# The order of helper calls in the eight attention turns, the last MLP and the recurrence periods, with the first and last rounds as functions of their own

## The reference

```python
x = L0(x, ctx)     # attention over channels, 64x64 weights, relu, residual
for w in (L1, L2): # two transformer layers
    q, k, v = split(layernorm(x) @ w_qkv + b_qkv)
    x = x + merge_heads(softmax(scores(q, k) * mask - 1e4 * (1 - mask)) @ v) @ w_ao + b_ao
    q = layernorm(x) @ w_q + b_q
    k, v = split(ctx @ w_kv + b_kv)
    x = x + merge_heads(softmax(scores(q, k) * cross_mask ...) @ v) @ w_co + b_co
    x = x + gelu(layernorm(x) @ w1 + b1) @ w2 + b2       # 256 -> 1024 -> 256
# L3: a recurrent block
xn = layernorm(x); sx = shifted(xn) - xn
x5 = xn + sx * (maa + tanh((xn + sx * maa_x) @ maa_w1) @ maa_w2)   # five mixes
w = exp(-exp(time_decay + tanh(x5[1] @ decay_w1) @ decay_w2))
r, k, v, g = x5[3] @ Wr, x5[0] @ Wk, x5[2] @ Wv, silu(x5[4] @ Wg)
s[t] = k[t] v[t]^T + w[t] * s[t-1];  out[t] = r[t] (u * k[t] v[t]^T + s[t-1])
x = x + groupnorm(out) * g @ Wo
x = x + sigmoid(xr @ ffn_Wr) * (relu(xk @ ffn_Wk)^2 @ ffn_Wv)
```

## Time and profile of the kernel before

| | us |
|---|---|
| three runs | 1107.12, 1105.58, 1101.60 |
| median | 1105.58 |
| the profiled execution | 1112.12 |
| its span in the trace | 1110.3 |
| granted clock of TensorE, mean of the span | 0.966 |

### The profile page before, as it was taken

The page is one execution under the profiler, slowest core; times in us unless marked ns, Lnnn a source line. Parts: engine busy times, 40 slices in busy tenths (PEclk is TensorE's granted clock), DMA queues, the critical chain, the costliest instruction groups (busy, mean ns, idle before and its releaser), DMA issues. The chain is left out here.

```text
span 1110.3 us, 24267 instructions
## 1 busy us (share of the span) xinstructions
PE 1022.3 (92%) x9312; PEld 697.3 (63%) x9312; DVE 772.5 (70%) x1517; ACT 517.6 (47%) x996; POOL 434.8 (39%) x387
## 2 busy tenths in 40 slices
PE   6998899999999999999999999998986889989966
PEld 4775676678677677677677678674462453644524
DVE  3674869757757757757757757754458898896964
ACT  4663463662662662662662662651411534414331
POOL 2111545443443443443443443431326536275240
PEclk9998899999999999999999999999998999989998
DMA  8230101001002002104001001210010010010100
GB/s 269 63 110 21 45 1 38 8 1 57 8 2 82 20 1 88 40 1 122 20 1 46 20 1 40 89 44 20 1 39 22 1 39 22 0 38 3 39 0 20
DMA packets 38002, 41.09 MB, mean 37 GB/s; under 512 B 8640, under 2 KB 33536, under 8 KB 37648
## 3 DMA queue, kind: packets, MB, share of 16 engines
q1 hardware_dynamic: 37776, 39.54, 11.2%
q0 software_dynamic: 128, 0.10, 0.0%
HBM read 31.25 MB, written 8.39 MB: 36 GB/s over the span
## 5 line engine op out<-in xcount | busy, mean ns | idle before, releaser
L2097 POOL TENSOR_TENSOR c_rs<-c_st,head_area 128x512 f32<-128x512 f32 x64 | 84.6, 1348 | 96.1 <-DVE c_st L2634 95.3
L792 POOL TENSOR_TENSOR head_area<-head_area,b_self_add 128x1024 f32<-128x1024 f32 x32 | 75.8, 2368 | 116.9 <-DVE head_area L1371 116.9
L792 POOL TENSOR_TENSOR head_area<-head_area 128x1024 f32<-128x1024 f32 x32 | 77.2, 2412 | 77.6 <-DVE head_area L1371 77.6
L1044 PE MATMUL ps<-b_hT_mlp,wl 128*128 128x512 f32 x224 | 107.0, 605 | 0.0
L1378 DVE TENSOR_REDUCE b_neg_max<-head_area 128x16 f32<-128x1024 f32 x64 | 77.6, 1212 | 34.1 <-POOL head_area L792 34.1
L1058 PE MATMUL ps<-w,b_act_g 128*128 128x256 f32 x448 | 100.9, 381 | 0.0
L1213 ACT ACTIVATE head_area<-head_area 128x1024 f32<-128x1024 f32 x64 | 67.9, 1061 | 63.8 <-DVE head_area L1383 63.7
L1218 ACT ACTIVATE head_area<-ps 128x512 f32<-128x512 f32 x128 | 69.9, 601 | 54.5 <-PE ps L991 54.5
L1058 PEld LDWEIGHTS ps<-w,b_act_g 128*128 128x128 f32 x448 | 83.5, 190 | 11.6 <-issue 1.0
L797 POOL TENSOR_TENSOR b_rstd<-b_var,minus_half 128x1 f32<-128x1 f32 x63 | 40.9, 649 | 124.8 <-DVE b_var L1407 124.1
L875 PE MATMUL ps<-head_area,wl 128*128 128x512 f32 x176 | 85.2, 613 | 3.2 <-issue 1.7
(11 more groups left out here) (262 smaller groups left out, 2138.3 us busy)
## 6 DMA issues: line engine op xcount, KB each, us to landing
head_area<-x_mid SPq DMA_DIRECT2D x9, 512.0 KB, 3.9
wl<-in_wl SPq DMA_DIRECT2D x4, 1024.0 KB, 6.8
head_area<-in_ctxT SPq DMA_DIRECT2D x8, 512.0 KB, 3.7
x_mid<-b_x_out SPq DMA_DIRECT2D x8, 512.0 KB, 3.5
area<-in_wc SPq DMA_DIRECT2D x1, 2336.0 KB, 9.3
a_x_in<-in_x SPq DMA_DIRECT2D x16, 128.0 KB, 2.5
a_y_in<-in_ctx SPq DMA_DIRECT2D x16, 128.0 KB, 3.5
w<-in_w SPq DMA_DIRECT2D x2, 1024.0 KB, 10.7
```

What stands on the lines that cost most here:

```text
L792: pool.tensor_tensor(t, t, m.unsqueeze(1).broadcast_to([P, NH, S]), ALU.add).then_inc(add_ok, 1)
L1044: mm = pe.matmul(ps[:, YB + j % 2, :], weight("w1", k, j * P, (j + 1) * P), hT_mlp[:, k, :], start=(k == 0), stop=(k == NC - 1))
L2097: pool.tensor_tensor(rs[:, i % BUFS, :], st[:, i % 3, :], rF[:, i // RS, :], ALU.mult).then_inc(rs_ok, 1)
```

## The change

No instruction that computes is added or taken away; operands and tiles are the same. What changes is the order of the calls, on PE, ACT, DVE and POOL. SP's stream of transfers is the same.

- `turn` has a new order on the four engines, and `first_turn` and `last_turn` are functions with orders of their own for turns 0 and 7.
- `last_mlp_first_head` has a new order on PE, ACT and DVE (POOL's is the same), in a function `work`.
- `period` has a new order on the four engines, and `last_head_period` and `last_period` are functions with orders of their own.
- `recurrence` and phase a are the same.

Core of the diff, PE at the end of the turn in the loop (shown in its state after; `-` and `+` mark places that moved):

```diff
                 times_v(n, 6)
                 next_scores(n, 6, nxt)
+                mlp_out(prev, 0, nxt)
                 last_project(n, 6, prev)
                 result_T(n, 6)
-                mlp_out(prev, 0, nxt)
+                mlp_out(prev, 1, nxt)
+                last_project(n, 7, prev)
 
                 probs_T(n, 7, nxt)
-                mlp_out(prev, 1, nxt)
-                last_project(n, 7, prev)
+                values_in(nxt, 1, prev)
                 times_v(n, 7)
-                values_in(nxt, 1, prev)
                 next_scores(n, 7, nxt)
                 mlp_out(prev, 2, nxt)
-                mlp_out(prev, 3, nxt)
                 result_T(n, 7)
+                mlp_out(prev, 3, nxt)
```

Last MLP and first head, PE and ACT:

```diff
-            low_rank()
-            hidden(0)
+                hidden(0)
+                low_rank()
...
-            to_tokens(vF, v_ok, FIRST_OUT["v_tok"])
-            hidden(7)
-            project(3, "r")
-            mlp_out(0)
-            project(4, "g")
-            for p in range(1, NP):
-                mlp_out(p)
+                mlp_out(0)
+                to_tokens(kF, k_ok, FIRST_OUT["k_tok"])
+                mix_pair(8)
+                project(2, "v")
+                mlp_out(1)
+                to_tokens(vF, v_ok, FIRST_OUT["v_tok"])
+                mlp_out(2)
+                project(3, "r")
+                project(4, "g")
+                mlp_out(3)
...
             low_rank_tanh()
+                gelu(0)
             decay_tanh()
             decays()
+                gelu(1)
             copy_projection("k", kF, k_ok)
...
-            gelu(0)
-            gelu(1)
             copy_projection("r", rF, r_ok)
```

More of the change, by code:

```diff
@@ L1074, in turn @@
             def turn(n, prev, nxt):
+                last_project(n, 0, prev)
                 keys_ctx(n, 0, prev)
+                probs_T(n, 0, nxt)
+                keys_ctx(n, 1, prev)
+                times_v(n, 0)
+                next_scores(n, 0, nxt)
+                values_ctx(n, 0)
+                result_T(n, 0)
+                probs_T(n, 1, nxt)
+                last_project(n, 1, prev)
+                values_ctx(n, 1)
+                times_v(n, 1)
+                next_scores(n, 1, nxt)
@@ new lines, in turn @@
+                norm_T_mlp(prev, n)
+                result_T(n, 1)
+                norm_T_mid(n, 0)
+                hidden(prev, 0, nxt)
+                queries_mid(n, 0)
+                hidden(prev, 1, nxt)
+                last_project(n, 2, prev)
+                probs_T(n, 2, nxt)
+                hidden(prev, 2, nxt)
+                times_v(n, 2)
+                next_scores(n, 2, nxt)
+                norm_T_mid(n, 1)
+                hidden(prev, 3, nxt)
+                queries_mid(n, 1)
@@ new lines, in turn @@
+                result_T(n, 2)
+                hidden(prev, 4, nxt)
+                last_project(n, 3, prev)
+                probs_T(n, 3, nxt)
+                hidden(prev, 5, nxt)
+                times_v(n, 3)
+                next_scores(n, 3, nxt)
+                norm_T_mid(n, 2)
+                norm_T_in(nxt, prev)
+                result_T(n, 3)
+                queries_mid(n, 2)
+                queries_in(nxt, 0)
+                last_project(n, 4, prev)
+                probs_T(n, 4, nxt)
@@ new lines, in turn @@
+                queries_in(nxt, 1)
+                times_v(n, 4)
+                next_scores(n, 4, nxt)
+                norm_T_mid(n, 3)
+                keys_in(nxt, 0)
+                queries_mid(n, 3)
+                result_T(n, 4)
+                keys_in(nxt, 1)
+                probs_T(n, 5, nxt)
+                hidden(prev, 6, nxt)
+                times_v(n, 5)
+                next_scores(n, 5, nxt)
+                last_project(n, 5, prev)
+                hidden(prev, 7, nxt)
+                probs_T(n, 6, nxt)
@@ L2103, in period, with last_period @@
+            def last_period(last, n, nxt):
+                tail, head, more = last is not None, n is not None, nxt is not None
+                if head: add_x(n, 0)
+                if head: add_x(n, 1)
                 if head: add_x(n, 2)
@@ new lines, in period @@
+                if tail: shift(1, last)
+                if tail: ffn_mix(last)
+                if head: key_value(n, 0, 0)
+                if head: key_value(n, 0, 1)
+                if head: key_value(n, 0, 2)
+                if more: shift(0, nxt)
+                if more: low_rank_in(nxt)
+                if head: key_value(n, 0, 3)
+                if head: key_value(n, 1, 0)
+                if head: key_value(n, 1, 1)
+                if head: own_weight(n)
+                if tail: result(last, (0,))
@@ new lines, in period @@
+                if head: key_value(n, 1, 2)
+                if tail: result(last, (1,))
+                if head: key_value(n, 1, 3)
+                if tail: result(last, (2,))
+                if tail: result(last, (3,))
+                if head: scan(n, 0)
+                if head: scan(n, 1)
+                if head: scan(n, 2)
+                if head: scan(n, 3)
+                if head: own_value(n, 0)
+                if head: scan(n, 4)
+                if head: scan(n, 5)
+                if head: scan(n, 6)
@@ L2701, in period, with last_head_period @@
+            def last_head_period(last, n, nxt):
+                tail, head, more = last is not None, n is not None, nxt is not None
+                if head: mixed(n, 0)
                 if head: mixed(n, 1)
```

979 lines of the change are left out of this document (804 added, 175 removed).

## The result

The changed kernel takes 1093.39 us (median of 8 runs, 1087.78 to 1098.43) against 1105.73 us (8 runs): ratio 0.9885, 95% interval 0.9853 to 0.9917. The forecast was 1092.8 us. In later runs it took 1096.3 us against 1105.67 (`x0_after`, ratio 0.9931, 0.9907 to 0.9955). The gain is 9 to 12 us by the medians, and 7.6 us by the later ratio. The total is as forecast, but its parts are not, as the stages show.

A forecast was written before the change was run, and what follows sets the result against it. PE was taken as full in phase b's loop, with engines waiting for one another outside it. Terms summed to -14.5 us, -12.8 with one low-clock stretch put back: 1105.6 us becomes 1092.8 us, range 1082 to 1104 us.

The forecast's parts named there:

- Turns 1 to 6: Loop of phase b: 0 us, ends -3 (idle time at the branch) and +5 (`mlp_out(0)` waiting for gelu 1).
- Turn 7: Last turn: -3.5 us, ends -5 and 0, from PE's waits at `norm_T_mid` (1.05 saved) and `times_v` (0.8 saved).
- Turn 0: First turn: -1.5 us, ends -4 and +2; covered waits give 2.5 us, `keys_ctx(1)` delays the first tile about 1 us.
- Last MLP: Last MLP and first head: -2.7 us, ends -4 and +1.5, from waits at `low_rank`, for gelu and for ACT's copies.
- Periods: Periods 0 and 1: -3.0 us each, net -1.2 from moving `own_weight`, 1.8 from DVE's idle time in the first half.
- Last head period: Last head period: -1.2 us, ends -3 and +1; moved `result` steps give -1.7, late `bonus` and `own_value` +0.5.
- Last period: Last period: +0.4 us, ends 0 and +1; a norm ahead of the last residuals delays norm 3 by one instruction.
- The one in which the periods give nothing: Rival, periods: POOL's pace already sets the scans and DVE's waits come back; sum -5.6, 1100.0 us; chance 0.18.
- The one in which waits only move: Rival, whole kernel: each wait goes and the same time is waited at the next one; 1105 us; chance 0.06.
- The slower one (gelu late in every turn): Rival, `mlp_out(0)` on PE in turns 1 to 6: 4.3 us six times, +25.7, 1118.5 us; chance 0.07.
- The one in which more goes than the waits: Rival, whole kernel: clock stays up for 5 us more, loop gives its 3; -20.8, 1084.8 us; chance 0.19.
- The stretch of low clock that I put back: Whole kernel: one new low-clock stretch, unseen by the walk, costs 1.7 us, taking the sum from -14.5 to -12.8 us.

The follow-up runs named there:

- x0_after: The changed kernel once more with no edit, against the kernel before run beside it: 1096.3 us, ratio 0.9931.
- x9_own_back: The changed kernel with `own_weight` behind scan 0 again, on DVE in the period of the loop alone: 1091.84 us, ratio 0.9893 to the kernel before.
- x5_one_turn: The changed kernel with one turn function, in the loop's new order, for all eight turns: 1109.73 us, ratio 1.0029 to the kernel before.
- x10_lh_own: The changed kernel with updates 12 and 13 first, and last head period's `own_weight` ahead of scan 0, r's projection and copy before update one: 1088.06 us, ratio 0.9858.
- x11_before: The kernel before once more, unchanged, for its trace: 1105.45 us, ratio 1.0002.

## Why the prediction was right, and where it was not

**The total** came out as forecast by terms that missed in both directions, and that they cancel is luck. At equal clock the orders are worth: turn 0 nothing, the loop -3 to -5, turn 7 -4.1 (and -1.6 where the stretch of low clock goes), last MLP -1.6 to -1.9, each period 0 to -1.2, last period -0.5 to +1.0; the last head period is open. The sum is between -8 and -15.5 us, and the two measurements of the changed kernel gave -12.3 and -9.4.

**Turns 1 to 6: wrong, and outside its bound.** The step set the idle time at the branch against a wait for gelu of 0 to 0.8 us a turn and took 0. The wait for gelu did not come: PE has no wait at L1132 in any turn. The waits at the branch did not go, they shrank by 1.2 us in five branches. The loop gave 0.8 us a turn, not 0.47 at most. The bound failed twice. It took the idle time of one turn (0.47 us) for all, while the six idle 3.9 us, 1.7 of it at the second branch. And it took PE's busy time for fixed, while that fell by 2.8 us (497.0 to 494.2) with the same matmuls. So the idle time of a window is no bound on what an order can give.

**Turn 7: right, too small.** The waits named went, down to 0.2 us; the step left 0.65 us at the norm of tile 3 and half of the smaller waits. The whole stretch of low clock went too, but the step's reason for it, that it stands behind the wait, is not borne out: with the old order of turn 7 the wait of 1.7 us was back and the stretch was not.

**Turn 0: wrong.** The walk covered 2.5 us of waits; in sum the chip covered none. The 1.7 us of the trace are the clock's.

**Last MLP: right, somewhat too large.** `hidden(0)` filled 0.6 us of the wait at `low_rank`, and the wait for gelu went, as worked out. The 1.35 us for copies covered by other work came to about 0.45, by subtraction: 1.8 less 0.6 and 0.75.

**Periods: one step of two.** That `own_weight` costs 1.41 us with POOL idle and no longer holds the scans was right, and so was the net: 1.4 us for a forecast of 1.2. The row of the kernel after:

```profile
881.17 1.41 DVE L3308 SCALAR_TENSOR_TENSOR head_area<-head_area,area 128x512 f32<-128x512 f32 x2
...
887.93 4.55 DVE L3328 TENSOR_TENSOR_SCAN c_st<-head_area,ps 128x512 f32<-128x512 f32 x4
...
903.46 1.22 DVE L3328 TENSOR_TENSOR_SCAN c_st<-head_area,ps 128x512 f32<-128x512 f32 x1 [0.71 <-ACT ps L3052]
```

`own_weight` (L3308) takes 1.41 us, the first four scans run on, and one late scan waits 0.71 us for ACT. The 1.8 us from DVE's idle time in the first half did not come; a share of an idle time without a named wait was no argument. The periods took 70.6 and 71.7 us, not 68 to 69. And an order with less slack pays for low clock that the old one hid: beside the scans it cost the new period 0.8 us (69.7 against 68.9 at 1.00) and wiped out nearly all of the gain there.

**Last head period: not settled.** 67.6 and 67.7 us are at equal clock but with the low stretches in different places. **Last period: not settled either.** Its new order took 38.6 to 38.9 us in eight traces against 37.9 before, but 37.4, 37.6 and 38.1 in `x9_own_back`, `x5_one_turn` and `x10_lh_own`, all with 13.7 us of low clock.

**The rivals.** The one in which the periods give nothing was nearest to the stages, and was made good by the loop and turn 7. The one in which waits only move is what turn 0 did, and no other stage. The slower one (gelu late in every turn) did not happen; where one turn function serves all turns, 1.1 us for gelu shows in turn 7. The one in which more goes than the waits had the loop right (-3), but its 5 us of clock were not reached: 1084.8 us lies below the fastest run of the changed kernel. The stretch of low clock that I put back (1.7 us) is not borne out: the first trace of the changed kernel has 13.7 us less low clock than that of the kernel before (61.4 against 75.1), `x11_before` and `x0_after` have 68.3 each, and where such stretches fall changes from run to run.

## What to carry to other kernels

An order tuned for a full loop body does not carry over to its first and last rounds, where calls are missing: used there, it cost 15 us, some of it in low clock, three times what it gave in the loop. Against the old order, ends of their own gave 4 us in turn 7 and nothing in turn 0. What stands last before a loop's branch should be long work that nobody waits for soon; a short piece that another engine copies for the next round's first call cost 3.7 us. Read every round's branch, for they differ by up to 1.8 us. Cost a reordering by the waits that have a name; a share of unnamed idle time is not a gain, and idle time is not a bound.
